# Batch 0's attention scores from float32 q and k on 32-row tiles instead of bf16 split stacks

## What is computed

```python
q = queries @ Wq.T + bq
k = queries @ Wk.T + bk
v = queries @ Wv.T + bv
q = q.reshape(Bq, L1, H, Dh).transpose(0, 2, 1, 3)      # H = 16, Dh = 16
k = k.reshape(Bq, L2, H, Dh).transpose(0, 2, 1, 3)
scores = jnp.einsum('bhqd,bhkd->bhqk', q, k) * scale + attn_mask[None]   # scale = 1/4
attn = jax.nn.softmax(scores, axis=-1)
heads = jnp.einsum('bhqk,bhkd->bhqd', attn, v)
```

## Time and profile before

| | us |
|---|---|
| median of 3 runs | 722.99 (721.27 to 723.14) |
| the profiled execution, its own time | 722.18 |
| its span, first to last instruction | 720.5 |
| PE busy / DVE busy | 622.3 / 602.0 |
| ACT busy / POOL busy | 566.9 / 505.9 |
| mean granted PE clock | 0.955 |
| DMA: HBM read / written | 28.73 MB / 4.26 MB |

### The profile page before, as it was taken

One profiled execution on the slowest core, in us unless ns is written; L12 is line 12 of the kernel. 1 busy time (PEld: TensorE's weight loads), 2 busy tenths in 40 slices (PEclk: granted clock), 3 DMA queues, 4 the chain that ended last, 5 costly groups with the idle time before them and its releaser, 6 DMA issues. The chain is left out here.

```text
span 720.5 us, 16641 instructions
## 1 busy us (share of the span) xinstructions
PE 622.3 (86%) x4892; PEld 451.7 (63%) x4892; DVE 602.0 (84%) x2387; ACT 566.9 (79%) x1189; POOL 505.9 (70%) x781
## 2 busy tenths in 40 slices
PE   5688998999999999999999999998988978684642
PEld 3465785777767676867686868676665746452311
DVE  2475798999999999999999999998979998685853
ACT  1165979899998989898989898988769687875531
POOL 3185678778897878888888888875968746644432
PEclk9599999999999999999999999999999999898856
DMA  8995939455556575647273737454194611111201
GB/s 237 142 214 119 131 76 137 98 89 123 85 104 103 104 105 101 106 93 114 78 113 83 115 66 132 70 100 79 57 131 82 115 42 46 21 61 37 73 16 44
DMA packets 106104, 69.20 MB, mean 96 GB/s; under 512 B 47200, under 2 KB 106016, under 8 KB 106016
## 3 DMA queue, kind: packets, MB, share of 16 engines
q1 hardware_dynamic: 106016, 68.14, 51.9%
HBM read 28.73 MB, written 4.26 MB: 46 GB/s over the span
## 5 line engine op out<-in xcount | busy, mean ns | idle before, releaser
L2774 DVE CUSTOM_DVE_ANT_0 sc<-pS,bias 128x256 f32<-128x256 f32 x512 | 198.5, 415 | 25.6 <-PE pS L291 18.4
L1444 POOL TENSOR_SCALAR sc<-sc,mx 128x256 f32<-128x256 f32 x336 | 166.5, 506 | 28.1 <-DVE mx L2774 27.0
L1895 ACT ACTIVATE pr<-pT 128x512 f32<-128x512 f32 x256 | 152.2, 614 | 16.4 <-PE pT L309 16.1
L309 PE MATMUL pT<-ident,sc 128*128 128x128 f32 x1024 | 152.9, 276 | 6.8 <-POOL sc L1444 3.8
L309 PEld LDWEIGHTS pT<-ident,sc 128*128 128x128 f32 x1024 | 118.0, 141 | 29.7 <-issue 14.7
L291 PE MATMUL pS<-ks,qs 96*128 96x256 bf16 x512 | 94.0, 275 | 7.8 <-DVE mx L2774 6.8
L1883 ACT ACTIVATE sc<-sc,mx 128x256 f32<-128x256 f32 x176 | 90.8, 528 | 3.5 <-DVE mx L2774 3.5
L291 PEld LDWEIGHTS pS<-ks,qs 96*128 96x128 bf16 x512 | 44.2, 98 | 42.6 <-DVE mx L2774 23.0
L326 PE MATMUL pO<-pr,va 128*32 128x256 f32 x1024 | 68.7, 386 | 0.6 <-ACT oT L1905 0.6
L1411 POOL TENSOR_TENSOR rs<-ve,minus_half 128x2 f32<-128x2 f32 x48 | 37.6, 782 | 33.1 <-DVE ve L2805 33.0
L1466 POOL TENSOR_SCALAR hq<-h 128x512 bf16<-128x512 f32 x64 | 38.5, 618 | 29.0 <-ACT h L2094 27.7
(11 more groups left out here) (291 smaller groups left out, 1672.9 us busy)
## 6 DMA issues: line engine op xcount, KB each, us to landing
qs<-parts SPq DMA_DIRECT2D x96, 128.0 KB, 4.7
ks<-parts SPq DMA_DIRECT2D x96, 128.0 KB, 4.9
mb<-mrows SPq DMA_DIRECT2D x16, 512.0 KB, 3.8
xin<-in_x SPq DMA_DIRECT2D x16, 256.0 KB, 3.6
xb<-in_x SPq DMA_DIRECT2D x16, 256.0 KB, 5.3
cx<-in_ctx SPq DMA_DIRECT2D x32, 128.0 KB, 2.1
out<-hq SPq DMA_DIRECT2D x16, 256.0 KB, 2.2
bias<-in_L_attn_pos_bias SPq DMA_DIRECT2D x4, 768.0 KB, 9.2
```

What stands on the lines that cost most here:

```text
L309: ins = pe.transpose(bank[:, kt * S + t * P:kt * S + t * P + P], sc[:, s % RING, t, kt * P:kt * P + P], ident[:])
L1444: ins = pool.tensor_scalar(sc[:, s % RING, t, :], sc[:, s % RING, t, :], -1.0, mx[:, s % RING, t:t + 1], ALU.mult, ALU.add)
L1895: act.activation(flat(pr[:, s % RING, :, :]), pT[s % 2][:, :], ACT.Exp, scale=-1.0)\
L2774: dve.tensor_tensor_reduce(out=sc[:, s % RING, t, :], in0=pS[s % 2][:, t * S:t * S + S], in1=bias[:, s, t * P:t * P + S][:, ::-1], scale=1 ...
```

## The change

Batch 0 goes another way from the projections to the scores; from batch 1 on the functions are as before. All five `opening()` lists are written anew; `body` and `closing` are unchanged.

- `weight_copied(0..3)` write into `y1` and `x1` with heads in blocks of 16 partitions; `weight_ordered(0..3)` (DVE, new) later make `wqT` and `wkT` from these, and `q_proj(1)`, `k_proj(1)` wait for them.
- `q_copy(0)` writes `y3`; `k_copy(0)` runs four activations instead of two and writes k twice, into `y2` with odd blocks of 16 partitions at zero, into `x2` with even ones at zero (`parity`, made by two small reductions of the identity, as the activation's scale). Four DMAs of the bias (`bq0`) and three small DVE instructions (`first_bias`) prepare their biases.
- `scores(0, s)`: two float32 matmuls with 32 partitions as contraction: two heads of q against one head of k, the other head's rows being zero.
- No split and no stack for batch 0: POOL loses `split_high(0, 0)` and `split_low(0, 0)`, DVE `k_split(0)`, SP 12 DMAs.
- PE's list before the first score is now: `weight_turned` 0 and 1, `x_turned(0)`, `weight_turned` 2 and 3, `q_proj(0)`, `k_proj(0)`. The other four `weight_turned`, `x_turned(1)`, `v_proj(0)`, `q_proj(1)`, `k_proj(1)`, `v_proj(1)`, `weight_mean(0)` stand among batch 0's scores. `weight_load(1)` stands behind batch 1's stacks on SP, `weight_signs(0)` behind `biased(0, 14, 1)` on DVE.
- Waits: `load_ctx(0)` waits for the memory settings on POOL; `exponentials(0, 2)` and `(0, 3)` wait for `weight_turned` 5 and 7, whose source they overwrite.

```diff
+        def first_k(s):
+            return (y2, x2)[s // KT % 2]
...
                 if s == 0:
-                    pe.wait_ge(stack.sem, stack.at(b, 16 * 12))
+                    if b == 0:
+                        pe.wait_ge(q_f.sem, 1)
+                        pe.wait_ge(k_f.sem, 1)
+                    else:
+                        pe.wait_ge(stack.sem, stack.at(b - 1, 16 * 12))
...
                 for t in range(TT):
+                    if b == 0:
+                        rows, m = slice(s // 4 * 32, s // 4 * 32 + 32), s % KT
+                        ins = pe.matmul(pS[s % 2][:, t * S:t * S + S], y3[rows, m, t * P:t * P + P],
+                                        first_k(s)[rows, m, :], start=True, stop=True)
+                        continue
...
             for i, r in enumerate((bq, bk)):
+                for m in range(KT):
+                    src = bass.AP(tensor=r.tensor, offset=m * DH, ap=[[KT * DH, NH // KT], [1, DH], [1, 1]])
+                    sp.dma_start(bq0[:, i * KT + m:i * KT + m + 1], src, allow_slow_non_contiguous=True).then_inc(d_q0.sem, 16)
+            load_bias(0)
...
             def opening():
                 weight_load(0)
-                load_stack(0, 0, 0)
-                load_stack(0, 0, 1)
-                weight_load(1)
                 load_bias(2)
                 load_bias(3)
+                load_ctx(0)
                 load_x(2, 0)
                 load_stack(1, 1, 0)
                 load_stack(1, 1, 1)
-                weight_load(2)
+                weight_load(1)
...
             def opening():
-                split_high(0, 0)
-                split_low(0, 0)
-                split_high(1, 0)
                 negated(0, 0)
...
+                negated(0, 5)
+                split_high(1, 0)
+                negated(0, 6)
+                split_low(1, 0)
+                negated(0, 7)
                 split_high(1, 1)
...
+                if b == 0 and 2 <= s < 4:
+                    act.wait_ge(p_set.sem, 2 * s + 2)
...
+                    for e in range(2):
+                        ins = act.activation((y2, x2)[e][:, m, :], src, ACT.Identity,
+                                             bias=k0_b[:, e * KT + m:e * KT + m + 1], scale=parity[:, e:e + 1])
...
+            def weight_ordered(k):
+                if k == 0:
+                    dve.wait_ge(v_set.sem, 4)
+                dve.tensor_copy((wqT, wkT)[k // KT][:, k % KT, :].rearrange("p (m r h) -> p m h r", m=KT, r=DH),
+                                (y1, x1[:, 0, :, :])[k // KT][:, k % KT, :].rearrange("p (m h r) -> p m h r", m=KT, r=DH))\
+                    .then_inc(w_ord.sem, 1)
```

More of the change, by code:

```diff
@@ L545, in opening @@
                 weight_turned(0)
+                weight_turned(1)
                 x_turned(0, 0)
-                weight_turned(1)
                 weight_turned(2)
                 weight_turned(3)
+                q_proj(0)
                 k_proj(0)
[L551 to L558, removed]
@@ L559, in opening @@
-                q_proj(1)
                 scores(0, 0, 0)
                 scores(0, 1, 0)
-                k_proj(1)
+                turned(0, 0)
                 scores(0, 2, 0)
                 scores(0, 3, 0)
+                turned(0, 1)
+                weight_turned(4)
                 scores(0, 4, 0)
+                weight_turned(5)
+                turned(0, 2)
                 scores(0, 5, 0)
[L567 to L570, removed]
+                x_turned(1, 1)
@@ L571, in opening @@
+                weight_turned(6)
+                weight_turned(7)
+                turned(0, 3)
                 scores(0, 6, 0)
[L572 to L576, removed]
+                v_proj(0)
                 scores(0, 7, 0)
                 scores(0, 8, 0)
+                q_proj(1)
+                k_proj(1)
+                v_proj(1)
+                weight_mean(0)
                 scores(0, 9, 0)
-                turned(0, 6)
@@ L581, in opening @@
-                turned(0, 7)
+                turned(0, 4)
                 scores(0, 10, 0)
                 scores(0, 11, 0)
+                scores(0, 12, 0)
+                turned(0, 5)
+                turned(0, 6)
                 x_turned(2, 0)
[L585 to L590, removed]
                 scores(0, 13, 0)
                 scores(0, 14, 0)
-                k_proj(2)
@@ L594, in opening @@
[L594 to L605, removed]
+                turned(0, 7)
+                turned(0, 8)
+                values(0, 0, 0)
+                scores(0, 15, 0)
@@ new lines, in opening @@
+                turned(0, 9)
+                values(0, 1, 0)
+                turned(0, 10)
+                turned(0, 11)
+                q_proj(2)
+                turned(0, 12)
+                values(0, 2, 0)
+                turned(0, 13)
+                turned(0, 14)
+                ctx_turned(0)
+                turned(0, 15)
+                scores(1, 0, 1)
+                scores(1, 1, 1)
+                values(0, 3, 0)
+                scores(1, 2, 1)
+                scores(1, 3, 1)
@@ L614, in opening @@
+                scores(1, 6, 1)
+                x_turned(3, 1)
                 turned(1, 2)
-                scores(1, 5, 1)
                 turned(1, 3)
[L617 to L620, removed]
                 scores(1, 7, 1)
+                x1_turned(0, 0)
                 turned(1, 4)
-                x1_turned(0, 0)
+                gate_parts(0)
+                gate_sums(0)
                 scores(1, 8, 1)
-                gate_parts(0)
+                values(1, 0, 1)
@@ L698, in opening @@
[L698 removed]
+                scores(3, 1, 1)
+                scores(3, 2, 1)
                 up_proj(0, 0)
+                turned(2, 10)
                 gate_proj(0, 1)
[L701 to L702 removed]
+                scores(3, 3, 1)
+                up_proj(0, 1)
+                turned(2, 11)
                 gate_proj(0, 2)
[L704 to L707 removed]
@@ L708, in opening @@
[L708 to L711, removed]
+                scores(3, 4, 1)
+                turned(2, 12)
+                gate_proj(0, 3)
+                turned(2, 13)
+                up_proj(0, 2)
+                turned(2, 14)
+                exponents_turned(1)
+                scores(3, 5, 1)
+                turned(2, 15)
+                scores(3, 6, 1)
                 values(2, 2, 0)
-                up_proj(0, 2)
@@ L750, in opening @@
                 down(0, 0)
                 gate_parts(2)
+                turned(3, 6)
+                gate_sums(2)
                 scores(3, 13, 1)
+                scores(3, 14, 1)
+                down(0, 1)
+                k_proj(5)
+                scores(3, 15, 1)
                 turned(3, 7)
-                gate_sums(2)
-                down(0, 1)
+                q_proj(5)
+                turned(3, 8)
                 values(3, 0, 1)
-                scores(3, 14, 1)
-                scores(3, 15, 1)
@@ L759, in opening @@
-                k_proj(5)
-                values(3, 1, 1)
-                turned(3, 8)
                 scores(4, 0, 0)
+                scores(4, 1, 0)
+                rows_turned(1)
                 turned(3, 9)
-                q_proj(5)
-                rows_turned(1)
-                scores(4, 1, 0)
                 scores(4, 2, 0)
-                turned(3, 10)
                 gate_proj(1, 0)
@@ L1414, in split_high @@
             def split_high(n, which):
-                if not live(n) or n == 0 and which == 1:
+                if not live(n) or n == 0:
                     return
```

659 lines of the change are left out of this document (335 added, 324 removed).

## The result

The changed kernel takes 733.59 us (median of 4 runs, 732.71 to 734.24) against 722.13 for the kernel before beside it: ratio 1.0142, 95% interval 1.0109 to 1.0175. It is 11.5 us slower where 11.9 us less were forecast. The first thing to look at is the page's header and its clock row.

What follows compares the result with a forecast made beforehand. PE was taken to set the loop's pace, so only its start could move: first score at 15.2, plus 30.1 work and 3.9 waits, puts batch 1 at 49.2 against 61.10; 722.18 - 11.9 = 710.3 us, range 703.5 to 716.0.

Steps and rivals of the forecast that it cites:

- batch 0 on PE: From first score to batch 1's: 28.1 us of listed work, 30.1 with changes of tile height, before waiting.
- a rival for one projection: k's projection before the first score takes 3.75 us, not 1.89; 712.2 us alone, part of the second rival's 0.25.
- The new start: Opening without k's split and stack: first score at 15.2 us, 19.6 before the old one.
- the two cases: k's projection in the opening takes 1.89 us, first score at 15.2, or 3.75, first score at 17.1.
- The score term: Batch 0 on PE: two float32 matmuls are 0.43 us for a head, 6.9 us for 16 heads.
- The waits: Batch 0 on PE keeps the old 3.9 us idle, as the hand-over between PE and DVE is the same.
- Second rival: Batch 0: PE's busy time is the better measure, 36.6 us, total 712.9; with its other causes, chance 0.25.
- The other two: Second rival's other causes: slow k projection, 712.2 us alone, and batch 1's stack as slow as batch 0's, 713.8.
- Third rival: Batch 0's scores: two float32 weight loads of 0.187 us per head show, adding 6.0 us: 716.3; chance 0.06.
- Fourth rival: `weight_signs(2)` on DVE waits for the later `weight_turn(0)`, holding up `biased` and PE: slower, 724.2 us if 2 us beyond; chance 0.04.
- Changing the tile height: PE in batch 0: 0.2 us per group of scores, about ten groups, 2.0 us.
- Batches 1 to 3 and the loop: After batch 0: PE has no more work, idle times of 3.4 and 3.6 us stay, loop periods 37.6 us as before.

Runs made afterwards that it cites:

- e1: Changed kernel with batch 0's score matmuls contracting over 128 partitions instead of 32, values wrong; 714.21 us, ratio 0.9873 to the kernel before.
- e3: Kernel before with batch 0's bf16 score matmuls cut to 32 of 96 partitions; 727.38 us in one run.
- e7: Changed kernel with batch 0's scores over 128 partitions, k masked with zeros, five masks on DVE, three on POOL; 712.07 us, ratio 0.9859 to the kernel before.
- e4: Changed kernel with nine extra full-height float32 matmuls between k's projection and the first score; 732.57 us.
- e10: Changed kernel with batch 0's scores over 128 partitions for heads 0 to 7 and 32 for heads 8 to 15; 721.92 us in one run.
- e5: Changed kernel with batch 0's scores over 128 partitions, k masked with zeros, one mask on DVE, seven on POOL; 721.84 us, ratio 0.9989.
- e2: Changed kernel with batch 0's score matmuls over 64 partitions instead of 32, values wrong; 722.75 us in one run.
- e6: Changed kernel with batch 0's scores over 128 partitions and a k of all zeros, values wrong; 713.08 us in one run.
- e9: Changed kernel with one more full-height float32 matmul ahead of each batch 0 head's two 32-row ones; 741.48 us in one run.
- e8: Changed kernel with consecutive heads of batch 0 on different groups of 32 rows, values wrong; 724.37 us in one run.

## Why the prediction was wrong

**What failed: the clock under the sum of batch 0.** The step "batch 0 on PE" priced every instruction at the upper clock, since in the kernel before the windows after the first score show 1.00. That price holds only as long as the clock stays where it was, and here it did not (0.64 over batch 0). The prediction had the clock as a rival for one projection (1.9 us), not for the stretch that it filled with a new kind of matmul. It is the term that carries the sign: with 128 rows 714.2, with 32 rows 733.6, the rest of the code the same. The windows from the first score to batch 1's, for the changed kernel and for e1 (granted clock 0.64 and 0.95), put it at 57.3 us where 34.0 were forecast, 30.1 of work and 3.9 of waits:

```profile
16.03:73.36 57.33, 57.32 (x240) 39.89 (x241) 21.17 (x80) 19.24 (x38) 19.87 (x32) 0.64 0.58 115
```

```profile
13.72:51.49 37.77, 37.76 (x240) 30.73 (x241) 21.30 (x80) 18.78 (x38) 19.75 (x31) 0.95 0.83 166
```

Of the 23.3 us too many, 19.6 go with the height, by e1, and nearly all of them with the clock: time multiplied by granted clock gives 36.7 us of work at the upper clock for the changed kernel and 35.9 for e1. The other 3.8 us lie in the sum itself, as follows.

**The new start** was nearly right: 16.03 against 15.2. q's projection started at 7.70 (7.8 said) and took 3.75; k's took 2.67, between the two cases. The prediction put the 3.75 down to the clock's lower level. A projection at granted 0.50 took 3.75 us as well (30.60 in the kernel before), but at the first one the granted clock reads 1.00 in both kernels, so the trace does not show that cause there. The bias did not hold the first `biased` up: it waited for PE's scores.

**The score term was also mis-sized.** I took a float32 matmul over 256 columns as 0.216 us, dividing 1.73 by the eight of a row. But `columns_by` and `rows_by` issue four matmuls each, two by two in loops, and not eight as the text ahead of the prediction has it; the trace has two records for each float32 matmul of 256 columns. (`values` likewise issues eight for its 16 records; its term was taken from the whole row and stands.) So one is 0.43 us, a head's two are 0.86, as e1 shows (26.42 to 27.28), and 16 heads cost 13.8 and not 6.9 us. A head's two bf16 matmuls step by 0.22 us in the kernel before (60.44 to 60.66), a quarter of that, where the expectation of e3 says half. The loop in the code, set beside the x8 of the row, would have shown it.

**The waits** were sized too high, which hid this in part. In e1, which has the lists of the change, PE was busy 37.76 of 37.77 us: it never waited where I had kept 3.9. My 28.1 us of work without the 2.0 for changes of tile height, which e1 does not have, plus the missing 6.9 is 35.0; 1.9 more are the lower clock at the first score rows of e1 (4.02 us from 13.72 to 17.74 for eight records and four transposes, against 1.73 and 0.44 at the upper clock), and 0.9 are left over. The forecast start of batch 1, 49.2, stands against 51.49 in e1 and 50.18 in e7, but that it comes so near is in part luck: from the first score to batch 1's it was 37.0 us in e7, not 34.0, and the first score stood at 13.14 and not at 15.2, since the two projections took 1.96 and 1.89 us there. With the clock held, the earlier start gives most of the gain that I had priced: the loop of e7 starts 11.5 us early where 11.9 were forecast.

**Second rival.** Its first cause, PE's busy time as the better measure, gave 36.6 us for batch 0, near the 37.8 of e1 and the 37.0 of e7; but it priced the dearer scores by the same halved matmul and kept the same 3.9 of idle time, so two errors offset each other. The other two were small or absent: the k projection cost 0.8 us too much, and batch 1's stack was no bound in the changed kernel, its last k part issued by 56.6 and PE not there before 73.

**Third rival, weight loads.** Refuted. In e4 heads 0 and 1 are both on the first 32 rows and run at the upper clock: eight matmul records in 1.99 us (its row at 16.92), 0.25 each at most, and the eight weight loads lie beside them:

```profile
16.92 1.59 PEld L302 LDWEIGHTS pS<-y 32*128 32x128 f32 x8 [0.33 <-issue]
```

A load of 0.187 that showed beside the 0.216 of a record would make each step 0.40.

**Fourth rival, slower by the turned weight.** The right sign by the wrong mechanism. `weight_turn(0)` was issued at 108.74, the last signs ran at 131.06, with no wait in front of them.

**Changing the tile height** costs a little more than was assumed: e10 puts one head alone on 32 rows between full-height matmuls, and from 26.48 to 28.49 it takes 2.01 us for two heads, where e1 takes 1.72 (26.42 to 28.14): 0.3 us for such a group, against 0.2 in the sum.

**Batches 1 to 3 and the loop** behaved as said: what was late at batch 1 (12.3 us) is late at the loop (11.8) and at the end (12.0), nothing was regained.

**Busy share and clock.** In the changed kernel PE was busy 9.00 of 9.00 us in each of the three windows from 17 to 44 us and had the lower level for most of them (0.50, 0.50, 0.72). The busy share that a profile shows is not enough to tell the clock: e1 has the same share (9.00, 9.00, 8.99) at 0.97, 1.00 and 1.00.

## What to carry to other kernels

Before making a matmul shorter in its contraction, ask what PE's clock will do: on a stretch where it is the bound, PE full with 32-row matmuls among its other work ran at a granted clock of 0.64 (57.3 us, the changed kernel), and the same number of score matmuls over 128 rows, most of them zeros, at 1.00 (37.0 us, e7) and at no higher cost for PE (two heads 1.73 us in e7, 16.36 to 18.09, against 2.00 over 32 rows in e10, 35.72 to 37.72); making the zeros cost DVE and POOL a multiplication for each pair of heads, and in e5 a badly placed one ate the whole gain. Look at the granted clock beside the busy share in every window; a busy PE at 0.50 is a loss that no list of waits shows. And count matmuls in the code before dividing a row of the trace by its x number.

## What the runs showed of the hardware that was not expected

- The clock fell with PE fully busy: at 37.7 us in e10 (0.52 from 38 to 39 us, PE busy 1.00 of 1.00), after four heads' 32-row scores with three full projections and some float32 transposes among them. 64 rows held it in the later part of batch 0 (e2, one run, 1.00 from 44 to 62 us); zeros over 128 rows held it (e6, one run, 1.00 from 17 to 71).
- With one full-height float32 matmul ahead of every two of 32 rows, a low clock stayed low from 17 to 44 us (0.50), and a high one stayed high from 47 to 80 (1.00; e9, one run).
- Two groups of 32 rows worked side by side: 1.14 us for two heads (e8) instead of 1.99 on one group (e4).
- POOL multiplied a 128x512 float32 tile by a per-partition scalar in 1.6 us (seven in 11.1, e5) while DVE needed 0.49 for the same (e5); POOL's conversion of such a tile to bf16 took 0.62 in the kernel before.
- After the same gap ahead of the first score, the clock was back near 17.74, after four 128-row score matmuls and four transposes (e1; 0.71 from 17 to 18 us, 1.00 after), and did not come back among the 32-row ones of the changed kernel (0.50 from 17 to 40 us). That it rose again near 40 us there (0.94 from 40 to 41), right after `v_proj`'s full-height matmuls, fits the height, but no run isolates it.
